# Finishing the state-space output in SBUF instead of in its PSUM bank

## The reference, cut to what matters

```
y    = scan(...)                          # 16 states, 512 channels, 512 steps
ssm  = (y + D*x) * silu(res)              # res: second half of W_in
out  = ssm @ W_out.T                      # [512, 256]
t    = normalised_x1 + alpha * out
x1   = x1 + t * silu(tree_output)         # stored as the result
```

## Time and profile before

| what | value |
|---|---|
| median of 3 runs | 3081.21 us (3074.79 to 3082.36) |
| profiled execution, its own time | 3081.21 us |
| its span, first to last instruction | 3079.4 us |
| mean granted TensorE clock | 0.906 |
| TensorE, VectorE, ScalarE, GpSimd busy | 81%, 64%, 60%, 56% of the span |

### The profile page before, as it was taken

One profiled execution on the slowest core, in us unless ns is written; L12 is line 12 of the kernel. 1 busy time (PEld: TensorE's weight loads), 2 busy tenths in 40 slices (PEclk: granted clock), 3 DMA queues, 4 the chain that ended last, 5 costly groups with the idle time before them and its releaser, 6 DMA issues.

```text
span 3079.4 us, 37563 instructions
## 1 busy us (share of the span) xinstructions
PE 2490.5 (81%) x12744; PEld 1392.3 (45%) x12744; DVE 1975.4 (64%) x2973; ACT 1851.8 (60%) x3344; POOL 1717.0 (56%) x1400
## 2 busy tenths in 40 slices
PE   5786689997788988998899779888888988957662
PEld 3444457764444444445444534453445444532321
DVE  4778645533356766676766656676766665769786
ACT  3457634346567675776677656766776657745552
POOL 1000155417556785777587748675866586545454
PEclk9888889998799989998999989999989989988886
DMA  4000268844454565545554544356434643455675
GB/s 139 21 18 5 77 171 248 239 134 69 85 137 90 100 141 131 104 94 124 131 106 84 127 103 101 74 110 141 100 77 99 143 95 82 103 130 132 142 159 112
DMA packets 281008, 344.83 MB, mean 112 GB/s; under 512 B 81456, under 2 KB 210366, under 8 KB 280816
## 3 DMA queue, kind: packets, MB, share of 16 engines
q0 software_dynamic: 79872, 171.99, 30.1%
q1 hardware_dynamic: 178432, 148.86, 16.5%
q10 hardware_dynamic: 22512, 21.57, 2.1%
HBM read 198.10 MB, written 26.80 MB: 73 GB/s over the span
## 4 chain that ended last, share of the span: by engine, by line
PE 45%; ACT 16%; DVE 14%; issue 12%; POOL 7%; SPq 3%; DMA 2%; another core or an unknown queue 0%; POOLq 0%; DVEq 0%; ACTq 0%
PE bank L1708 7%; PE bank L1697 7%; PE bank L1847 4%; PE bank L1659 4%; PE bank L1818 4%; PE bank L1766 3%; PE bank L1876 3%; POOL acc_sb L1572 3%; DVE bank L1491 3%; PE bank L1720 3%; POOL arena L1588 3%; ACT PT L986 2%; ACT bank L1092 2%; ACT Pr L966 2%; SPq L786 2%
## 5 line engine op out<-in xcount | busy, mean ns | idle before, releaser
L1588 POOL TENSOR_TENSOR arena<-arena 128x512 f32<-128x512 f32 x512 | 849.2, 1719 | 123.5 <-DMA arena<-bc_dram 103.8
L1491 DVE TENSOR_TENSOR_SCAN bank<-bank,arena 128x512 f32<-128x512 f32 x320 | 391.4, 1223 | 230.6 <-ACT bank L1092 199.7
L1572 POOL DMA_INDIRECT acc_sb<-ybuf,slot_idx x256 | 421.9, 1648 | 179.4 <-DMA ybuf<-arena 63.0
L1594 POOL TENSOR_TENSOR arena<-arena 128x512 f32<-128x512 f32 x192 | 277.9, 1447 | 387.3 <-DVE arena L1491 348.2
L1092 ACT ACTIVATE bank<-arena,A_sb 128x512 f32<-128x512 f32 x512 | 352.5, 693 | 202.3 <-DVE arena L1499 188.8
L1697 PE MATMUL bank<-Kp,Qp 64*128 64x512 f32 x1024 | 413.7, 683 | 73.0 <-ACT Pr L966 69.0
L1708 PE MATMUL bank<-ident,Pr 128*128 128x128 f32 x2048 | 353.8, 298 | 133.4 <-ACT PT L986 79.9
L966 ACT ACTIVATE Pr<-bank,negmax 128x512 f32<-128x512 f32 x512 | 353.6, 691 | 154.8 <-DVE negmax L1184 125.9
L1184 DVE TENSOR_REDUCE negmax<-bank 128x1 f32<-128x512 f32 x512 | 343.0, 679 | 160.9 <-PE bank L1697 160.2
L986 ACT COPY PT<-bank 128x512 f32<-128x512 f32 x512 | 299.7, 585 | 213.9 <-PE bank L1708 195.5
L1708 PEld LDWEIGHTS bank<-ident,Pr 128*128 128x128 f32 x2048 | 229.2, 148 | 312.2 <-issue 90.8
(11 more groups left out here) (211 smaller groups left out, 3895.5 us busy)
## 6 DMA issues: line engine op xcount, KB each, us to landing
arena<-arena POOLq DMA_DIRECT2D x256, 512.0 KB, 5.4
arena<-bc_dram SPq DMA_DIRECT2D x256, 256.0 KB, 4.1
ybuf<-arena ACTq DMA_DIRECT2D x64, 256.0 KB
arena<-in_w_gate SPq DMA_DIRECT2D x64, 128.0 KB
arena<-in_w_up SPq DMA_DIRECT2D x64, 128.0 KB
arena<-in_w_down SPq DMA_DIRECT2D x64, 128.0 KB
arena<-in_X SPq DMA_DIRECT2D x8, 512.0 KB, 7.3
s_sb<-in_X SPq DMA_DIRECT2D x8, 512.0 KB, 9.4
```

The costliest lines, as they stand in the source:

```text
L1491: dve.tensor_tensor_scan(v if c_by_pool(m) else decay, decay, v, 0.0, ALU.mult, ALU.add).then_inc(ssm_scan, 1)
L1572: pool.indirect_dma_start(acc_sb[:, i, :], None, ybuf, bass.IndirectOffsetOnAxis(ap=slot_idx[:, b * TILES + i, k:k + 1], axis=0), bounds_c ...
L1588: pool.tensor_tensor(st_sb[:, g % RING_S, :], u_sb[:, size_slot(b, cb), :], B_sb[:, load % RING_BC, :], ALU.mult).then_inc(ssm_input, 1)
L1594: pool.tensor_tensor(v, v, C_sb[:, load % RING_BC, :], ALU.mult).then_inc(ssm_c_pool, 1)
```

## The change

Three VectorE instructions of `ssm_fin` write and read `fin_sb` in SBUF where they wrote and read the PSUM bank. The first still reads the matmul's result from the bank; the second and the third have no operand in PSUM any more. Since the bank is then free after the first instruction of a tile, three waits of TensorE on the counter `ssm_fin` (three counts a tile) are lowered: the wait of the second `ssm_out` of a tail by two counts, and the waits of `ssm_h` (b of 2 and more) and of `ssm_res` (last sequence) by two counts.

```diff
             def ssm_fin(self, b, i):
-
-                o, sl = bank[SIDE][:, i % 2 * DM:(i % 2 + 1) * DM], b % 2
+                fin, sl = fin_sb[:, i, :], b % 2
                 at = 3 * (TILES * b + i)
...
-                dve.scalar_tensor_tensor(o, o, alpha_sb[:, 0:1], fin_sb[:, i, :], ALU.mult, ALU.add).then_inc(ssm_fin, 1)
+                dve.scalar_tensor_tensor(fin, bank[SIDE][:, i % 2 * DM:(i % 2 + 1) * DM], alpha_sb[:, 0:1], fin, ALU.mult, ALU.add).then_inc(ssm_fin, 1)
...
-                dve.tensor_tensor(o, o, g1[:, i, :], ALU.mult).then_inc(ssm_fin, 1)
+                dve.tensor_tensor(fin, fin, g1[:, i, :], ALU.mult).then_inc(ssm_fin, 1)
...
-                dve.tensor_tensor(x1[:, sl, i, :], o, x1[:, sl, i, :], ALU.add).then_inc(ssm_fin, 1)
+                dve.tensor_tensor(x1[:, sl, i, :], x1[:, sl, i, :], fin, ALU.add).then_inc(ssm_fin, 1)
...
             def ssm_h(self, b, c):
-                    w.wait_ge(ssm_fin, 3 * TILES * (b - 1))
+                    w.wait_ge(ssm_fin, 3 * TILES * (b - 1) - 2)
...
             def ssm_res(self, b, cb):
-                    w.wait_ge(ssm_fin, 3 * TILES * b)
+                    w.wait_ge(ssm_fin, 3 * TILES * b - 2)
...
             def ssm_out(self, b, pair):
-                    w.wait_ge(ssm_fin, 3 * (TILES * b + 2 * pair))
+                    w.wait_ge(ssm_fin, 3 * (TILES * b + 2 * pair - 1) + 1)
```

## The result

The changed kernel takes 3102.92 us (median of 6 runs, 3102.33 to 3111.75), the kernel before 3076.08 us (6 runs, 3074.20 to 3082.36). The ratio is 1.009, with a 95% interval of 1.0074 to 1.0105: 23 to 32 us slower, 27 by the medians. The forecast was 3098.3 us with a range of 3079 to 3111. It counted from 3081.2 us, the median of the three runs then at hand, and six runs have 3076.08 us; so the change itself was forecast at +17.1 us and measured at +27. Of the other ends that it named, 3084, 3079, 3071 and 3120 us, none is near the measured time.

A forecast was written before the change was run, and what follows sets the result against it. The chain was taken to run through VectorE's `ssm_fin` in 14 of 16 half-tails, with TensorE waiting behind it. GpSimd waits 17.0, release -1.9 and clock +2 made +17.1 us on 3081.2: 3098.3 us, range 3079 to 3111.

The forecast's parts named there:

- Second and third instruction, with GpSimd at work: In `ssm_fin`, VectorE instructions with two SBUF tensors stand still until GpSimd's instruction is through: +17.0 us.
- the upper bound of 35: Mean excess of disturbed rows, 0.63 us, on all 56 second and third `ssm_fin` instructions before the final tail: 35 us.
- The rule: If GpSimd's L1588 or L1594 is open when a second or third instruction would start, it ends 0.31 us after that.
- The nine half-tails that were priced: Half-tails on the chain with GpSimd at such an instruction: delays of 0.0 to 4.5 us each, +17.0 us in sum.
- First instruction and undisturbed ones at 0: In `ssm_fin`, the first stays at 482 ns; the second and third without GpSimd change by -0.1 us, taken as 0.
- One for one to the end: `ssm_fin` time on VectorE counts nearly one for one, since the chain passes through it in 14 of 16 half-tails.
- Release at -1.9 us: At the second `ssm_out` of the last two tails, TensorE starts 0.94 and 0.95 us sooner by the earlier bank release.
- Clock at +2 us: Longer TensorE stalls behind `ssm_fin` bring one or two more stretches at clock 0.50: +2 us, ends 0 and 6.
- Swallowed waits: Rival: waits behind GpSimd come but a quarter of the 17 us arrives: +2.4, 3084 us; chance 0.25.
- No effect of GpSimd's: Rival: at this width instructions slip between GpSimd's or it stays out of step; only the release remains, 3079 us; chance 0.10.
- The release working in all eight tails: Rival: TensorE gains 0.94 us at each second `ssm_out`, 7.5 us, and 3 us from shorter stalls: 3071 us; chance 0.04.
- The extreme: Rival: VectorE loses to two GpSimd instructions each time and most stalls end in the lower clock: +39, 3120 us; chance 0.06.

The follow-up runs named there:

- the turns: Changed kernel, with GpSimd also waiting at its place in the order until `ssm_fin` of both tiles of a half-tail is done: 1.0022 of the kernel before.
- the twins: Kernel before plus an unneeded fourth `ssm_fin` VectorE instruction per tile: 1.0124 with both tensors in SBUF, 1.0048 with one in PSUM.
- the twin: Kernel before plus an unneeded fourth `ssm_fin` VectorE instruction per tile, with one tensor in PSUM and one in SBUF: 1.0048.
- the two profiles: Two profiled executions of the unaltered changed kernel, the second later on another chip: 3116.98 and 3097.58 us.

## Why the prediction was right, and where it was off

- *Second and third instruction, with GpSimd at work.* The mechanism was as laid out, and the turns and the twins show it. The size was 17.0 us and measured 31.0, nearly the upper bound of 35. Two things were off. The rule let an instruction in after the GpSimd instruction that was open; in half-tail one that gave 4.1 us where 6.7 were measured, in the fifth 4.5 for 5.4, in the ninth 1.7 for 3.0. The nine half-tails that were priced came to 23.1 us in place of 17.0. And three were put at nothing: the second, taken as undisturbed, had 1.6 us, and the seventh and eighth, near 2066 before and taken as off the chain, 5.0 and 1.5 us. In the chain after, these two are on it, so that their delay outgrew the slack.
- *First instruction and undisturbed ones at 0.* Right: 475 ns and a median of 425.
- *One for one to the end.* Right within what can be told: 15 us for 14 of plain VectorE time in the twin. For the change, 31.0 and 35 us of excess in the two profiles, less 1.9, stand beside 32.8 and 29.5 us from the first `ssm_fin` on and 27 us by the medians. So little was swallowed, and the sum is good to a few us only.
- *Release at -1.9 us.* Right for TensorE's start in both tails (-0.94 and -0.95). In the next to last one only 0.4 us of it went on: from the first to the second half it was 6.21 us instead of 6.60, since the second half then stood behind VectorE's own L1499 and L1491. A third tail was added, that of the fourth sequence. In time the release alone is not resolved by taking it back; put in where GpSimd is idle it gives -4 us, with an interval that holds -1.9.
- *Clock at +2 us.* Of the two stretches looked at one grew, by some 1.3 us of time. The total stays open. From the first `ssm_fin` on, the matmuls of the two profiles are busy 1544.1 and 1544.6 us, 6 to 7 us more than the 1537.7 before; but with the release taken back they are busy 1534.1 us, and that run lost as much.
- *The rivals.* Swallowed waits: no, see above. No effect of GpSimd's: no. The release working in all eight tails: no, in three, and at 0.9 us each it could only give back part of what VectorE had lost. The extreme: its size of the term (35 us) was nearer than mine, its clock part was not seen.

So the sum of 17.1 us had a term too small by 14 and, against it, some 4 us that did not arrive: with the +2 for the clock it would have been 31, and the medians say 27. The size was off by 10 us; 3098.3 lies within 5 us of the measured 3102.92 only because the kernel before had been taken 5 us too long. That part is luck.

## What to carry to other kernels

Before an operand of a VectorE instruction is moved out of PSUM, look at what GpSimd does at that place: the PSUM operand may be what keeps the two engines apart. A group whose minimum and median are alike while the mean is far above tells of such meetings; find them in the timelines of both engines. Where VectorE is on the chain and GpSimd is not, a wait that makes GpSimd stand back for a short VectorE instruction can be cheap: it gained 10 us at `ssm_xs`, and left 7 us of the loss at `ssm_fin`. Try it, since the average slack of an engine is not its slack at one place.

## What the runs showed that I had not expected

A VectorE instruction with both tensors in SBUF doesn't always take the next turn. With GpSimd instructions ready one behind the other it stood through two or three of them, up to 5.63 us for 0.43 us of work. Nor does it help to be first by a little when GpSimd is in the middle of something: L1518 started at 2086.24, 0.29 us before L1587 (2086.53), while GpSimd's L1571 was running, and took 3.63 us. With GpSimd idle before, 0.16 us ahead had been enough. Was it the running L1571, a gather, that kept VectorE out? One L1520 ran beside such a gather alone and took its usual 0.43 us:

```profile
1181.47 0.43 DVE L1520 TENSOR_TENSOR x<-x,arena 128x256 f32<-128x256 f32 x1
...
1181.31 1.63 POOL L1571 DMA_INDIRECT acc_sb<-ybuf,slot_idx  x1 [0.16 <-issue]
```

So that isn't likely, but the records don't show when a waiting GpSimd instruction was ready. The Trainium skill, page "SBUF — State Buffer", section "SBUF: two separate sides", says that whichever starts first gets the pair of ports that the two engines share for the whole instruction. By the records' start times that does not hold in the cases of 1182.32 and 2086.24, and the measurement decides.
